# Inverse square roots of four groups moved from GpSimd to a Newton batch on VectorE

## The chip, the cores and the metric

The kernel runs on one core of a Trainium2 chip. The metric is the device time of one execution in microseconds, the median of several runs. TensorE is written PE in the profile, VectorE DVE, ScalarE ACT, GpSimd POOL and SyncE SP.

## The reference

`x` is 16 x 256 rows of 128 numbers (4096 rows). Three layers follow one another, all in float32:

```python
x = x + 0.5 * ffn(layernorm(x))
x = x + attn(layernorm(x))
x = x + 0.5 * ffn(layernorm(x))

# layernorm: (x - mean) / sqrt(var + 1e-5), over the 128 numbers of a row
# ffn: logits = x @ router.T, one of 8 experts by argmax;
#      y  = (silu(x @ gate_e.T) * (x @ up_e.T)) @ down_e.T    (the row's expert, hidden width 256)
#      ys = the same with the shared expert's weights, for every row;  y + ys
# attn: circular convolution with a key, decaying sum over the 256 rows of a sequence,
#       circular correlation with a second key; x + gate * result
```

## The kernel before

The 4096 rows are 32 tiles of 128 rows, in eight groups of four tiles (`G` = 8, `TPG` = 4). The two feed-forward layers are numbered f = 0 and f = 1. Each has a loop over the groups that normalizes, routes and sends the rows out, and then a loop over 39 blocks of 128 rows of one expert each (`experts`).

**The opening (f = 0).** Every engine runs its own program and they meet at semaphores. Step k of `front(0, k)` does this. VectorE chooses the expert of each row of group k from the router's product (`choose`, L646 to L652); between the links of that chain it places the first half of the statistics of group k + 3 (`moments`, L575), and behind it their end (`aggregate`, L582 to L586). TensorE then counts ranks (L924 to L932), and VectorE turns them into the row's slot (`place_rows`, L661 and L665). GpSimd sends each tile of the group to its slots by an indirect DMA (`scatter`, L391), four to a group. GpSimd also turns variances into inverse square roots, by a power of minus a half (`rstd`, L376), and makes the shift from it (L380): groups 0, 1 and 2 ahead of the first scatter, groups 3 and 4 in one instruction ahead of the scatters of group 1, 5 and 6 ahead of those of group 3, and 7 ahead of those of group 4. ScalarE copies the transposed rows out of PSUM (L475), normalizes the next group (`norm`, L460), and does the SiLUs (L484). TensorE's order in step k is: a piece of the shared expert, the router's product for group k (L902), another piece, the transposes of group k + 1 (L867), the ranks of group k.

**The shared expert** is cut into pieces `(g, part)`: parts 0 and 1 are the two halves of gate and up of group g (L881 on TensorE, the SiLU L484, the product `mult` L623 on VectorE), and part 2 (`DOWN`) the down product (L889) and its addition to the rows (`add_shared`, L591). They are worked off in the order of `SHARED_PARTS`: none in step 0, two in each of the steps 1 to 7 (`PER_STEP`), five behind the last step (`parts_left`), and the last five, (6,1), (7,0), (6,2), (7,1), (7,2), behind the loop over blocks.

**The end of the opening.** VectorE writes `pad_row` (L729) behind the slots of group 7 and then makes the tables of blocks (L742 to L768). SyncE writes eight blocks of pads to the rows that `pad_row` names (L331), and waits for the tables, all pads and all 32 scatters (L336) before it loads the first blocks (L320).

**Preparing the attention** (`prepare_attention`, L831 to L839; a product L1000 on TensorE; a Tanh L551 on ScalarE) stands in step 0.

**Behind the blocks of f = 0.** SyncE waits for all rows that GpSimd returned and loads them into `back`. VectorE does the products of (6,1) and (7,0) and the addition of (6,2), then in `middle(-4)` adds `back` of group 0 (L591), takes its statistics for the attention, and does the product of (7,1); in `middle(-3)` it does the same for group 1, and then the addition of (7,2). `middle(-2)` begins with the scan of group 0 (L603). TensorE does its five pieces and then the transposes for that scan (L867), which need ScalarE's normalized rows (L460).

## Time and profile before

| | |
|---|---|
| median of 3 runs | 306.56 us (306.52 to 307.95) |
| the profiled execution | 306.67 us, its span 304.9 us |
| mean granted TensorE clock | 0.924 of full speed |
| busy, share of the span | PE 85%, DVE 60%, POOL 57%, ACT 53% |

Times in a profile count from the start of the span; the profiled execution's own time is 1.8 us longer than its span. A timeline row gives start, duration, engine, line and operation, what is written and read, how many instructions are merged in the row, and in brackets the idle time ahead of it and what ended that. `issue` is time in which an engine waited for nothing that the profile shows.

### The profile page before, as it was taken

Reading aid. Unit: us, or ns where it says so; the run is one execution under the profiler, and the core shown is the slowest. Engines: PE = TensorE matmul, PEld = TensorE weight load, DVE = VectorE, ACT = ScalarE, POOL = GpSimd, SP = SyncE. Lnnn points to the kernel's source line nnn. Section 1 sums busy time; section 2 is a strip of 40 time slices with the busy share of each in tenths; the row PEclk is TensorE's granted clock in tenths of the full one; section 3 lists DMA queues with packets and bytes.
Section 4 is the critical chain, followed back from the end, with each engine's and each line's share of the span. In section 5 each row is a group of like instructions: output and inputs, shape, how many; then the busy total and the mean of one; then the engine's idle time right before and its main releaser. Section 6 shows DMA issues by size and latency. Waiting matters only on the chain.

```text
span 304.9 us, 6662 instructions
## 1 busy us (share of the span) xinstructions
PE 259.1 (85%) x1802; PEld 213.1 (70%) x1802; DVE 184.4 (60%) x752; ACT 160.4 (53%) x374; POOL 172.7 (57%) x223
## 2 busy tenths in 40 slices
PE   8789999839999999857698999999940999999980
PEld 2457677529999999636465676666620899999980
DVE  4647656724566556357999788784471266666650
ACT  2635542226777677118485776654202477767730
POOL 6467787701667667713543667665653047477673
PEclk9899999978999999996597999999995699999996
DMA  6961112433333321054000111121263835444110
GB/s 198 342 256 48 42 47 64 141 80 75 89 92 93 83 63 43 30 153 123 0 2 1 53 41 49 71 72 70 72 211 108 212 93 148 132 113 136 38 54 9
DMA packets 27060, 28.56 MB, mean 94 GB/s; under 512 B 4711, under 2 KB 23533, under 8 KB 26768
## 3 DMA queue, kind: packets, MB, share of 16 engines
q1 hardware_dynamic: 21968, 17.51, 20.5%
q0 software_dynamic: 5056, 10.63, 10.2%
q8 instruction: 15, 0.25, 0.4%
q14 instruction: 21, 0.17, 0.2%
HBM read 15.70 MB, written 13.34 MB: 95 GB/s over the span
## 4 chain that ended last, share of the span: by engine, by line
PE 54%; POOL 15%; issue 12%; DVE 9%; DMA 6%; ACT 3%; POOLq 0%; SPq 0%; DVEq 0%; ACTq 0%
PE bank L956 21%; PE bank L881 10%; POOL dispatched L391 9%; PE bank L966 9%; PE bank L889 5%; PE bank L947 3%; PE bank L908 2%; PE bank L902 2%; DVE scanned L603 2%; POOL returned L418 2%; POOL scale_f L376 2%; DMA dispatched<-rows,slot 2%; DVE st_f L575 1%; POOL out L418 1%; DMA xs<-dispatched 1%
## 5 line engine op out<-in xcount | busy, mean ns | idle before, releaser
L956 PE MATMUL bank<-xsT,wgu 128*128 128x128 f32 x624 | 86.1, 283 | 1.2 <-ACT xsT L530 1.2
L391 POOL DMA_INDIRECT dispatched<-rows,slot x64 | 63.1, 987 | 30.8 <-issue 18.3
L956 PEld LDWEIGHTS bank<-xsT,wgu 128*128 128x128 f32 x624 | 79.2, 199 | 1.7 <-issue 1.7
L881 PE MATMUL bank<-xnT,gu 128*128 128x512 f32 x128 | 64.2, 629 | 2.2 <-DVE hs L623 1.8
L800 DVE TENSOR_TENSOR eh<-eg,bank 128x256 f32<-128x256 f32 x78 | 32.9, 422 | 46.1 <-ACT eg L537 45.5
L418 POOL DMA_INDIRECT out<-ey,token x39 | 38.3, 981 | 30.6 <-DVE ey L809 19.8
L418 POOL DMA_INDIRECT returned<-ey,token x39 | 38.3, 982 | 30.5 <-DVE ey L813 18.1
L509 ACT ACTIVATE wgu<-gu 128x512 f32 x78 | 48.3, 624 | 9.7 <-DVE tab_row L768 6.3
L484 ACT ACTIVATE sg<-bank 128x512 f32<-128x512 f32 x32 | 19.0, 593 | 56.6 <-PE bank L881 56.6
L966 PE MATMUL bank<-wdn,eh 128*128 128x128 f32 x312 | 47.1, 276 | 0.8 <-DVE ey L809 0.4
L537 ACT ACTIVATE eg<-bank 128x256 f32<-128x256 f32 x78 | 29.9, 383 | 33.2 <-PE bank L956 32.5
L966 PEld LDWEIGHTS bank<-wdn,eh 128*128 128x128 f32 x312 | 40.8, 192 | 1.1 <-DVE eh L800 1.1
L889 PEld LDWEIGHTS bank<-dn,hs 128*128 128x128 f32 x256 | 32.3, 201 | 12.5 <-DVE hs L623 8.5
L889 PE MATMUL bank<-dn,hs 128*128 128x128 f32 x256 | 33.5, 287 | 5.9 <-DVE hs L623 5.9
L881 PEld LDWEIGHTS bank<-xnT,gu 128*128 128x128 f32 x128 | 22.8, 197 | 20.6 <-issue 19.6
L460 ACT ACTIVATE rows<-rows,shift_f,scale_f 128x128 f32<-128x128 f32 x64 | 26.3, 484 | 14.6 <-POOL shift_f L380 14.6
L947 PE MATMUL bank<-ident,xs 128*128 128x128 f32 x78 | 16.6, 291 | 14.4 <-DMA xs<-dispatched 14.4
L777 DVE COPY wdn<-dn 128x256 f32 x78 | 23.5, 303 | 5.6 <-issue 4.6
L623 DVE TENSOR_TENSOR hs<-sg,bank 128x512 f32<-128x512 f32 x32 | 21.8, 681 | 8.1 <-ACT sg L484 8.0
L376 POOL TENSOR_TENSOR scale_f<-var_f,minus_half 128x4 f32<-128x4 f32 (+1 forms) x14 | 15.6, 1113 | 12.2 <-DVE minus_mean_f L586 12.1
L902 PEld LDWEIGHTS bank<-routerT,xnT 128*128 128x128 f32 x128 | 16.2, 194 | 7.7 <-issue 3.9
L947 PEld LDWEIGHTS bank<-ident,xs 128*128 128x128 f32 x78 | 10.8, 152 | 15.2 <-issue 14.5
(99 smaller groups left out, 299.8 us busy)
## 6 DMA issues: line engine op xcount, KB each, us to landing
xs<-dispatched SPq DMA_DIRECT2D x39, 130.0 KB, 2.2
xs<-dispatched SPq DMA_DIRECT2D x39, 66.0 KB, 2.1
gu<-in_gu SPq DMA_DIRECT2D x1, 2048.0 KB, 10.8
back<-returned SPq DMA_DIRECT2D x8, 256.0 KB, 5.3
dispatched<-pads SPq DMA_DIRECT2D x9, 130.0 KB, 3.0
dn<-in_dn SPq DMA_DIRECT2D x1, 1024.0 KB, 11.6
dispatched<-rows,slot POOLq DMA_INDIRECT x64
returned<-ey,token POOLq DMA_INDIRECT x39, 2.3
```

What stands on the lines that cost most here:

```text
L391: nc.gpsimd.indirect_dma_start(dispatched[f][:, :], bass.IndirectOffsetOnAxis(slot[:, i:i + 1], 0), rows[:, i, 0:width(f)], None, bounds_c ...
L418: nc.gpsimd.indirect_dma_start(target, bass.IndirectOffsetOnAxis(token[:, b % TR:b % TR + 1], 0), ey[:, b % YR, :], None, bounds_check=las ...
L460: nc.scalar.activation(dst[:, at * TPG + t, 0:C], xres[:, i, :], ACT.Identity, bias=shift[kind][:, i:i + 1], scale=scale[kind][:, i:i + 1] ...
L509: nc.scalar.activation(wgu[:, b % GR, :], tile(gu, expert_of(digits[0], b)), ACT.Copy).then_inc(blk_wgu, 1)
L537: nc.scalar.activation(eg[:, b % GR, :], bank[4 + b % GR][:, 0:H], ACT.Silu).then_inc(blk_silu, 1)
L777: nc.vector.tensor_copy(wdn[:, b % WR, :], tile(dn[:].rearrange("p e h c -> p e (h c)"), expert_of(digits[0], b))).then_inc(blk_wdn, 1)
L800: nc.vector.tensor_tensor(eh[:, b % WR, :], eg[:, b % GR, :], bank[4 + b % GR][:, H:2 * H], ALU.mult).then_inc(blk_mul, 1)
L881: last = nc.tensor.matmul(ps[:], gu[:, SHARED, at:at + P], xnT[:, g, :], start=True, stop=True)
L889: last = nc.tensor.matmul(o_ps[:, t * C:(t + 1) * C], hs[:, n % 2, h, t * P:(t + 1) * P], dn[:, SHARED, h, :], start=(h == 0), stop=(h == ...
L947: last = nc.tensor.transpose(bank[q % 2][:, i * P:(i + 1) * P], xs[:, b % XR, 0:C], ident[:])
L956: last = nc.tensor.matmul(bank[4 + b % GR][:, c * P:(c + 1) * P], wgu[:, b % GR, c * P:(c + 1) * P], xsT[:, b // 2 % TURNS, b % 2, :], sta ...
L966: last = nc.tensor.matmul(bank[2 + b % 2][:, 0:C], eh[:, b % WR, h * P:(h + 1) * P], wdn[:, b % WR, h * C:(h + 1) * C], start=(h == 0), st ...
```

## The change

Groups 4 to 7 of the opening no longer get their inverse square roots from GpSimd's power. VectorE computes all sixteen columns at once behind the slots of group 2: a first guess from the bits of the number, three Newton steps of three instructions, and the shift, twelve instructions in a chain, each waiting for the one before. GpSimd keeps groups 0 to 3, all ahead of its first scatter. For this the statistics of group 5 move into step 1, and those of groups 6 and 7 into step 2 (`STATS_AT`). ScalarE's `norm` of groups 4 to 7 waits for the whole chain. The attention's preparation moves from step 0 to step 3 (`PREPARE_AT`) on all engines, and TensorE waits for the shared weights behind the router's product of group 0 instead of ahead of it. `FILL` gives the same two pieces to each step as `PER_STEP` did. The last five pieces (`REST`) keep their order; on VectorE the product of (7,1) now stands ahead of `middle`, and the addition of (7,2) in `middle(-4)`.

```diff
+STATS_AT = {-3: (0,), -2: (1,), -1: (2,), 0: (3,), 1: (4, 5), 2: (6, 7)}
+BY_DVE = 4
+NEWTON = 3
+MAGIC = float(0x5F3759DF)
+DVE_RSTD_STEPS = 3 + 3 * NEWTON
+SHARED_FROM = 1
+PREPARE_AT = 3
...
-PER_STEP = 2
-EARLY = PER_STEP * (G - 1)
+FILL = (0, 2, 2, 2, 2, 2, 2, 2)
+EARLY = sum(FILL)
 LATE = EARLY + 5
+REST = SHARED_PARTS[LATE:]
+REST_DVE = {-4: REST[4:6], -3: REST[6:7], -2: REST[7:]}
...
             def first_ffn(k):
                 if k < 0:
-                    rstd("f", k + AHEAD, k + AHEAD)
-                elif k in (1, 3):
-                    rstd("f", k + 2, k + 2, groups=2)
-                elif k == 4:
-                    rstd("f", k + 3, k + 3)
-                if valid(k):
+                    rstd("f", k + BY_DVE, k + BY_DVE)
+                else:
                     scatter(0, k)
...
-                act.wait_ge(rstd_done[kind], (n + 1) * RSTD_STEPS)
+                if kind == "f" and BY_DVE <= n < G:
+                    act.wait_ge(dve_rstd, DVE_RSTD_STEPS)
...
+            def rstd_of_rest():
+
+                at = slice(BY_DVE * TPG, NT)
+                v, y, step = var["f"][:, at], scale["f"][:, at], [0]
+
+                def link(ins):
+                    step[0] += 1
+                    ins.then_inc(dve_rstd, 1)
+                    if step[0] < DVE_RSTD_STEPS:
+                        dve.wait_ge(dve_rstd, step[0])
+
+                dve.wait_ge(stats["f"], G)
+                link(nc.vector.tensor_scalar(square[:].bitcast(I32), v.bitcast(I32), 1, None,
+                                             ALU.logical_shift_right))
+                link(nc.vector.tensor_scalar(y.bitcast(I32), square[:].bitcast(I32), -1.0, MAGIC, ALU.mult, ALU.add))
+                for _ in range(NEWTON):
+                    link(nc.vector.tensor_tensor(square[:], y, y, ALU.mult))
+                    link(nc.vector.scalar_tensor_tensor(out=square[:], in0=square[:], scalar=-0.5, in1=v,
+                                                        op0=ALU.mult, op1=ALU.mult))
+                    link(nc.vector.scalar_tensor_tensor(out=y, in0=square[:], scalar=1.5, in1=y,
+                                                        op0=ALU.add, op1=ALU.mult))
+                link(nc.vector.tensor_tensor(shift["f"][:, at], y, minus_mean["f"][:, at], ALU.mult))
...
                 if valid(k):
                     place_rows(n, k, q)
+                for more in laters[1:]:
+                    stats_of(kind, more, more)
+                if f == 0 and k == max(STATS_AT):
+                    rstd_of_rest()
...
-                if k < -2:
-                    shared(0, *SHARED_PARTS[k + 2])
+                for g, part in REST_DVE.get(k, ()):
+                    shared(0, g, part)
...
-                if k == 0:
+                if k == PREPARE_AT:
                     prepare_attention()
...
-            for g, part in SHARED_PARTS[LATE:-2]:
+            for g, part in REST[:4]:
                 shared(0, g, part)
...
             pe.wait_ge(routes_in, 16)
+            for k in range(0, SHARED_FROM):
+                front(0, k)
             pe.wait_ge(shared_in, 16 * 2)
-            front(0, 0)
+            for k in range(SHARED_FROM, PREPARE_AT + 1):
+                front(0, k)
             pe.wait_ge(small_in, 16 * 4)
```

## Rows read from the trace of the kernel before

**Rows 1.** Timeline of GpSimd in the opening: powers and scatters.

```profile
13.39 1.20 POOL L391 DMA_INDIRECT dispatched<-rows,slot  x1 [2.17 <-DVE slot L665]
...
19.90 1.67 POOL L376 TENSOR_TENSOR scale_f<-var_f,minus_half 128x8 f32<-128x8 f32 x1 [1.48 <-DVE minus_mean_f L586]
...
22.41 1.07 POOL L391 DMA_INDIRECT dispatched<-rows,slot  x1 [0.49 <-issue]
...
39.85 1.05 POOL L376 TENSOR_TENSOR scale_f<-var_f,minus_half 128x4 f32<-128x4 f32 x1
...
41.34 1.05 POOL L391 DMA_INDIRECT dispatched<-rows,slot  x1 [0.16 <-issue]
...
59.28 0.97 POOL L391 DMA_INDIRECT dispatched<-rows,slot  x1 [0.30 <-issue]
```

**Rows 2.** Chain that ended last, 0 to 75 us: start, us, what.

```profile
60.55 2.32 DMA dispatched<-rows,slot
...
66.83 2.05 PE bank L956 x8
```

**Rows 3.** Timeline of VectorE and TensorE in steps 0 to 3 of the opening.

```profile
12.61 0.17 DVE L586 TENSOR_SCALAR minus_mean_f<-mv_f 128x4 f32<-128x4 f32 x1
...
12.74 3.45 PE L881 MATMUL bank<-xnT,gu 128*128 128x512 f32 x4
...
26.28 0.19 DVE L665 TENSOR_REDUCE slot<-place 128x4 int32<-128x32 f32 x1
...
28.22 1.96 PE L881 MATMUL bank<-xnT,gu 128*128 128x512 f32 x4
...
31.28 2.05 PE L889 MATMUL bank<-dn,hs 128*128 128x128 f32 x16 [0.51 <-DVE hs L623]
...
31.36 0.19 DVE L665 TENSOR_REDUCE slot<-place 128x4 int32<-128x32 f32 x1
```

**Rows 4.** Timeline of VectorE: a choice without statistics, and a piece of the tables.

```profile
44.36 0.19 DVE L646 TENSOR_REDUCE top<-bank 128x4 f32<-128x32 f32 x1 [1.59 <-PE bank L902]
...
45.64 0.68 DVE L623 TENSOR_TENSOR hs<-sg,bank 128x512 f32<-128x512 f32 x1
...
55.91 0.20 DVE L762 SCALAR_TENSOR_TENSOR blk_row<-block_no,blk_from 128x40 f32<-128x40 f32 x1
...
56.14 0.20 DVE L764 TENSOR_TENSOR packed<-blk_exp,digit 128x40 f32<-128x40 f32 x1
```

**Rows 5.** The pads: timeline of `pad_row`, and line 331 from 48 to 62 us.

```profile
51.74 0.16 DVE L729 TENSOR_TENSOR pad_row<-bank,pad_base 128x8 int32<-128x8 f32 x1
...
L331 SPq DMA_DIRECT2D dispatched<-pads x8: 332/332/354, 53.9 to 58.1; - x8
...
DMA to landing us min/median/max: 1.9/2.3/2.6
```

**Rows 6.** Stretches of 1 us: PE, PEld, DVE, ACT, POOL, clock, DMA.

```profile
13.00:14.00 1.00, 1.00 (x2) 0.33 (x1) 0.91 (x5) 0.42 (x2) 0.61 (x1) 0.50 1.05 442
...
136.00:137.00 1.00, 0.00 (x0) 0.00 (x0) 0.93 (x9) 0.00 (x0) 0.00 (x0) 0.50 0.95 266
...
163.00:164.00 1.00, 1.00 (x5) 0.60 (x4) 1.00 (x8) 0.66 (x2) 0.00 (x0) 0.55 0.02 8
```

**Rows 7.** Timeline behind the first blocks, 133 to 143 us.

```profile
133.59 0.60 ACT L484 ACTIVATE sg<-bank 128x512 f32<-128x512 f32 x1 [2.91 <-PE bank L881]
134.63 0.69 DVE L591 SCALAR_TENSOR_TENSOR rows<-back,rows 128x512 f32<-128x512 f32 x1 [2.06 <-DMA back<-returned]
...
136.82 0.68 DVE L623 TENSOR_TENSOR hs<-sg,bank 128x512 f32<-128x512 f32 x1
...
137.56 3.79 PE L889 MATMUL bank<-dn,hs 128*128 128x128 f32 x16 [4.00 <-DVE hs L623]
...
138.51 1.65 ACT L460 ACTIVATE xa<-rows,shift_a,scale_a 128x128 f32<-128x128 f32 x4 [4.32 <-POOL shift_a L380]
...
142.24 1.22 DVE L603 TENSOR_TENSOR_SCAN scanned<-keep,bank 128x512 f32<-128x512 f32 x1 [0.16 <-PE bank L867]
```

More of the change, by code:

```diff
@@ L137, in build @@
         scale_more = sb("scale_more", [P, NT])
+        square = sb("square", [P, (G - BY_DVE) * TPG])
         top = sb("top", [P, TPG])
@@ L252, in parts_at @@
             if f == 0:
-                return SHARED_PARTS[PER_STEP * (k - 1) + i:][:1] if 1 <= k < G else []
+                if not valid(k):
+                    return []
+                first, middle = sum(FILL[:k]), (FILL[k] + 1) // 2
+                return SHARED_PARTS[first + i * middle:first + (FILL[k] if i else middle)]
             if not valid(k):
@@ L368, in _, with rstd @@
             last_token = pool.to_reg(N - 1)
-            def rstd(kind, n, k, groups=1):
-                s, w = rstd_done[kind], groups * TPG
-                at = slice(k * TPG, k * TPG + w)
-                pool.wait_ge(stats[kind], n + groups)
+            def rstd(kind, n, k):
+                s = rstd_done[kind]
+                at = slice(k * TPG, (k + 1) * TPG)
+                pool.wait_ge(stats[kind], n + 1)
+                if kind == "f" and n >= G:
+                    pool.wait_ge(dve_rstd, DVE_RSTD_STEPS)
+                    n -= G - BY_DVE
                 sc = scale[kind][:, at]
-                nc.gpsimd.tensor_tensor(sc, var[kind][:, at], minus_half[:, 0:w], ALU.pow).then_inc(s, 1)
+                nc.gpsimd.tensor_tensor(sc, var[kind][:, at], minus_half[:], ALU.pow).then_inc(s, 1)
                 pool.wait_ge(s, n * RSTD_STEPS + 1)
@@ L442, in _ @@
             pool.wait_ge(const_made, 3)
-            for k in range(-AHEAD, 1):
-                first_ffn(k)
-            for k in range(1, G):
+            for k in range(-BY_DVE, G):
                 first_ffn(k)
@@ L556, in _, with middle @@
             experts(0)
-            for g, part in SHARED_PARTS[LATE:]:
+            for g, part in REST[:6]:
                 shared(0, g, part)
-            steps(lambda k: front(1, k), 3)
+            def middle(k):
+                front(1, k)
+                for g, part in REST_PE.get(k, ()):
+                    shared(0, g, part)
+            steps(middle, 3)
             before_experts(1)
@@ L668, in front @@
                 n, q = f * G + k, k % 2
-                kind, later = ("f", k + AHEAD) if f == 0 else ("a", k + 4)
+                kind, laters = ("f", STATS_AT.get(k, ())) if f == 0 else ("a", (k + 4,))
+                later = laters[0] if laters else G
                 if f == 0 and valid(later):
@@ L718, in middle @@
                 front(1, k)
-                if k < -2:
-                    shared(0, *SHARED_PARTS[k + 2])
+                for g, part in REST_DVE.get(k, ()):
+                    shared(0, g, part)
             def pads_behind(f):
@@ L1006, in _, with middle @@
             experts(0)
-            for g, part in SHARED_PARTS[LATE:]:
+            for g, part in REST[:6]:
                 shared(0, g, part)
             pe.wait_ge(setup, 6)
-            steps(lambda k: front(1, k), 3)
+            def middle(k):
+                front(1, k)
+                for g, part in REST_PE.get(k, ()):
+                    shared(0, g, part)
+            steps(middle, 3)
             for g, part in parts_left(1):
```

14 lines of the change are left out of this document (10 added, 4 removed).

## The prediction

> **What bounds the kernel now.** I read the chain of waits first, for the opening. From about 20 to 61 us it is one unbroken run of GpSimd scatters: each takes 0.97 us plus 0.30 us until the next [rows 1], so 32 of them need 41 us. Three times the run is broken by an inverse square root of L376. Group 0's four scatters (first at 13.39) are out at about 18.5, but the next starts at 22.41, behind the 1.67 us power of groups 3 and 4: 3.9 us. The same power stands once more at 32.4 (2.2 us lost), and the one at 39.85 costs 1.2 us [rows 1]. Together that is 7.3 us, and it is what the change goes for. The last scatter's rows land at 62.87, and only then does SyncE load the experts' first blocks [rows 2].
>
> Next, the order of time on TensorE and VectorE, because a scatter also needs its slots. Slots of group 2 are written at 26.47, those of group 3 at 31.55 [rows 3]; GpSimd without its powers would want group 3's at about 31. So this second chain (gate-up, router product, gate-up or down, transposes, ranks, slots: about 5.0 us a step) is almost as late as GpSimd. A third one hangs on it: VectorE's pad rows at 51.74, then SyncE's eight pad writes from 53.9 to 58.1, each landing 2.3 us after its issue (1.9 to 2.6), the last at 60.4 [rows 5]. SyncE waits for pads and scatters alike. The opening can therefore give at most 62.87 - 60.4 = 2.5 us, whatever GpSimd gains, unless the slots come earlier, and the change doesn't make them earlier.
>
> Last, the stretch after the first experts, where the diff also moves two VectorE pieces: it is bound by a chain of waits through `back`, VectorE, TensorE and the first scan [rows 7].
>
> **The change part by part.** *GpSimd.* Three powers leave it; the one of group 3 now stands ahead of the first scatter. Its statistics are ready at 12.77 [rows 3]; from power to scatter takes 1.49 us, as from 39.85 to 41.34 [rows 1], which puts the first scatter at 14.4 in place of 13.39. Cover: group 1's slots come at 20.7, four scatters end at 19.6, so this costs nothing.
>
> *Steps 0 to 2.* The attention's preparation leaves step 0, where VectorE had been idle behind it. It frees TensorE by 0.3 us; group 2's slots go from 26.47 to about 26.1. Group 5's statistics move into step 1 and group 6's into step 2, group 7's behind the slots of step 2: 1.49 us for a group (136.82 less 134.63 + 0.70) [rows 7].
>
> *Newton steps.* Twelve dependent instructions on 128x16. The trace has none of that width. From below: six linked steps of a choice take 1.28 us (44.36 to 45.64), 0.21 each; from above: the table's chain steps by 0.23 us (55.91 to 56.14) on 40 columns [rows 4]. I take 0.21, so 2.5 us (range 2.5 to 2.8). They have no cover: VectorE is at 26.1 with group 2's slots, 27.6 with group 7's statistics, and 30.1 with the last shift. Behind them wait, on VectorE, the add of group 0 (0.6) and the choice of step 3, which TensorE has had ready since 28.0; on ScalarE, the normalizing of group 4, and queued behind it both SiLUs of step 3; on TensorE, the transposes of group 4 and all that follows. In numbers: choice 30.7 to 32.0; ScalarE normalizes 30.1 to 31.7 (1.65 [rows 7], the next can start 0.1 sooner), SiLU to 32.2; product to 32.95; slots of group 3 at 33.4 instead of 31.55; the down product of group 1, which waits for that product, at 33.0 instead of 31.28 [rows 3]. So the slot chain is 1.7 us later, and GpSimd idles from 31.2 to 33.7.
>
> *TensorE's clock.* Between the gate-up of step 3 (28.22 before [rows 3], now about 27.9, done in 2.0) and 33.0 TensorE has only four transposes and the ranks: a hole of 3.3 us. The trace shows what such holes do. The granted clock is at half (1.2 GHz) at 13, after sparse small work; at 136, 2.4 us after 133.6; and at 163 after a stretch that was only thinned by waits [rows 6]. At half, a group of four gate-up products takes 3.45 us [rows 3] instead of 1.96 [rows 3], and the low stretches that were filled with work lasted about 3.4 us (13 to 16.4). I charge one such stretch: 1.7 us more on the slot chain. From the down product (31.28) to the pad rows (51.74) TensorE is the pace and nothing there is changed but the preparation (1.6 us of VectorE at step 3, hidden while TensorE does the down product and the router). So the pad rows stand at 33.0 + 20.46 + 1.7 = 55.1, the last pad at 63.8 less 0.2 for a wait on ScalarE in step 4 that goes: 63.5. GpSimd's last scatter lands at about 62. The gate for the experts is now the pads, at 63.5: **+0.65** against 62.87. Without the fall it is 61.8: -1.1.
>
> *Start of the experts.* Blocks begin at 66.83 at the half clock, 2.05 us for eight matmuls [rows 2]. TensorE's leftover products now end 3.2 us later, so the fall comes later, and less of the blocks' work is done slow. Between 0 and 2.0; I take **-0.35**, which lets the low stretch end where it ended.
>
> *Statistics, choice and shared parts later.* Steps 3 and 4 have no statistics left; VectorE isn't the pace there. Zero. The wait for the shared weights moves behind the first router product: they had landed, zero.
>
> *After the experts.* `REST` has five parts; by its slices the product (7,1) now stands before the first add of `back`, and the add of group 7 behind the first statistics instead of behind the second add. Before, the SiLU of (7,1) is ready at 134.19, VectorE idles until `back` comes (134.63, 2.06 us idle), adds, does statistics, and multiplies only at 136.82; TensorE, its clock down, takes 3.79 us for the down product from 137.56; its queue holds the transposes for the scan behind that, though their input is ready at 140.16; the scan starts at 142.24 [rows 7]. Now: product 134.2 to 134.9, `back` added 0.2 later, down product 134.9 to 137.7 at the latest, its add on VectorE 0.7, which lies in VectorE's wait. The transposes follow ScalarE: 140.4, scan at 140.75. **-1.5**. From the scan to 154.6 VectorE is the chain, without a gap, then TensorE; both keep the 1.5.
>
> Sum: 0.65 - 0.35 - 1.5 = -1.2 against the profiled execution's 306.67 (span 304.9 plus 1.8): 305.5. The median is 0.1 lower: **305.4**.
>
> **The rivals.**
> - *No fall of the clock in the hole* (A). For it: the transposes and ranks lie in the hole. Then -1.1 at the gate, and TensorE is so close behind its leftover work that the experts may start at the full clock: -1.1 - 0.35 to -1.1 - 2.0, and -1.5: 302.0 to 303.6, say 302.6.
> - *A low stretch elsewhere falls away* (B). The one at 163 lies in a part that TensorE bounds; 1.2 us of shift can give its sparse moment more work. 305.4 - 1.7 = 303.7. As well one can be added: 307.1 (B').
> - *The moved product gives nothing* (C): `back`, not the product, could hold the scan through ScalarE. 305.4 + 1.5 = 306.9. Against it: 2.1 us between ScalarE's 140.16 and the scan.
> - *Slower: Newton's steps are held up beside the scatters* (D). Group 2's scatters run during them. The nearest rows say no: 0.2 us steps and 0.97 us scatters stand side by side in the tables' chain [rows 1, 4]. From above: if a step could run only in the 0.30 us between scatters, 2.5 us would become up to 10.7. The price is one to one on slots and pads. From 2.7 us more the kernel is over 308.1; I put it at 309.
> [...]
> - *The change does what it is for* (E): slots keep pace, opening -2.5, 302.6 with the rest. The 2.5 us of uncovered Newton speak against it.
>
> **How the numbers follow.** Forecast 0.34 (own range 304.6 to 306.4); A 0.13; B 0.17; B' and C 0.19, of it 0.06 for both at once (308.6); D 0.12, of it 0.09 above 308.1; E 0.05. Range: 302.5 to 307.7; what is left out is D, B' with C, and the lower edge of A and E. Half a per cent, about what a measurement of this kernel tells from no change, is 1.5 us: 305.0 to 308.1. Faster: A, B, E and a sixth of the forecast: 0.41. Slower: 0.09 and 0.06, 0.15. Same: 0.44.
>
> **What would show it.** Right: no L376 between scatters; twelve steps in 2.5 us; scatter of group 3 near 33.7 after an idle of 2.4 us; granted clock at half for one stretch after about 33; the last pad, not the last scatter, releasing the first block load, at 63 to 64; the scan 1.5 us nearer to the landing of `back`. Wrong: steps of over 0.3 us (D), full clock through 33 to 37 (A), a scan that comes as late as before behind `back` (C), a missing low stretch past 160 (B).

## The result, and the profile after

| | before | changed |
|---|---|---|
| median (us) | 306.66 | 311.07 |
| lowest to highest | 306.52 to 307.95 | 309.58 to 312.04 |
| profiled execution, span | 306.67, 304.9 | 312.04, 310.3 |
| mean granted clock | 0.924 | 0.904 |

The changed kernel takes 1.0137 of the time before, 95% interval 1.0088 to 1.0186: it is slower by 1.4%. A second set of runs gave 310.97 against 307.03, 1.0112 (1.0069 to 1.0155). The forecast was 305.4, with a range up to 307.7. Ratios, here and below, leave out executions more than 1.5% above the fastest of the same kernel, so a ratio is not the quotient of the two medians (they lie up to 0.5% apart).

I cut both executions at events that both have, which shows where the time came in. The third kernel is the changed one once more, profiled in the second set (`e5_changed_again`). It matters because the first step of the opening differs between executions without any cause in the code.

| us | before | changed | changed again |
|---|---|---|---|
| slots of group 1 written | 20.7 | 22.8 | 21.0 |
| slots of group 2 | 26.5 | 28.2 | 26.7 |
| group 2 to group 3 | 5.1 | 7.2 | 7.2 |
| group 3 to group 4 | 5.7 | 7.0 | 8.7 |
| slots of group 7 written | 51.8 | 57.2 | 57.3 |
| from there to the first block load | 11.2 | 10.0 | 9.9 |
| first block load | 63.07 | 67.14 | 67.21 |
| from there to the load of `back` | 68.6 | 69.2 | 68.2 |
| load of `back` to the first scan | 10.6 | 9.3 | 9.3 |
| first scan to fifth scan | 29.6 | 31.8 | 31.7 |
| fifth scan to the end of the span | 133.1 | 132.8 | 132.6 |

Against "changed again" the span grows by 4.1: 4.1 at the gate of the experts, -0.4 in the blocks, -1.3 to the scan, +2.1 behind it, -0.5 in the rest. Against the first execution of the changed kernel it is 5.4. There 2.1 us more than before stand at the slots of group 1 already, ahead of everything that the Newton steps could delay.

The page of the changed kernel: TensorE's busy tenths and its granted clock, in 40 slices of 7.8 us.

```profile
PE   7799899959999999885698999999960799999990
...
PEclk9759799995999999998558999999995599999996
```

The clock row of the page before, in slices of 7.6 us:

```profile
PEclk9899999978999999996597999999995699999996
```

The clock row is lower in the second, third and fifth slices (11.7 to 21.9 and 35.5 to 39.0 us), and from 145 to 162 us. Now the opening itself. VectorE, ScalarE and TensorE in the timeline of the changed kernel (start, length, engine, line, operation, tile; in brackets the idle time ahead and what ended it):

```profile
28.01 0.19 DVE L711 TENSOR_REDUCE slot<-place 128x4 int32<-128x32 f32 x1
...
29.70 0.18 DVE L624 TENSOR_SCALAR square<-var_f 128x16 int32<-128x16 int32 x1
29.91 0.17 DVE L626 TENSOR_SCALAR scale_f<-square 128x16 int32<-128x16 int32 x1
...
32.00 0.17 DVE L633 TENSOR_TENSOR shift_f<-scale_f,minus_mean_f 128x16 f32<-128x16 f32 x1
...
32.21 1.65 ACT L477 ACTIVATE rows<-rows,shift_f,scale_f 128x128 f32<-128x128 f32 x4 [4.15 <-DVE shift_f L633]
...
35.11 3.40 PE L940 MATMUL bank<-dn,hs 128*128 128x128 f32 x16 [0.40 <-DVE hs L669]
...
35.19 0.19 DVE L711 TENSOR_REDUCE slot<-place 128x4 int32<-128x32 f32 x1
```

The Newton chain runs from 29.70 to 32.17, twelve steps that start 0.21 us apart. ScalarE waits 4.15 us for its last product. The down product behind it takes 3.40 us, where it took 2.05 before [rows 3]: the fall of the clock has come. Slots of group 3 are written at 35.38, 7.2 us behind those of group 2.

GpSimd in the same timeline (it answers to [rows 1]):

```profile
28.47 0.97 POOL L409 DMA_INDIRECT dispatched<-rows,slot  x1 [0.56 <-DVE slot L711]
...
35.65 0.97 POOL L409 DMA_INDIRECT dispatched<-rows,slot  x1 [2.39 <-DVE slot L711]
...
42.70 0.97 POOL L409 DMA_INDIRECT dispatched<-rows,slot  x1 [2.26 <-DVE slot L711]
...
55.51 0.97 POOL L409 DMA_INDIRECT dispatched<-rows,slot  x1 [2.90 <-PE bank L953]
...
64.54 0.97 POOL L409 DMA_INDIRECT dispatched<-rows,slot  x1 [0.30 <-issue]
```

In [rows 1] powers stand between the scatters; here there are none, and GpSimd idles instead. It waits 2.39 and 2.26 us for slots and then 2.90 us for something else: a router product of TensorE (L953). The last scatter starts at 64.54, and in the chain of waits it is this one that the block loads follow, no pad (start, length, what; it answers to [rows 2]):

```profile
64.54 2.40 DMA dispatched<-rows,slot
...
70.85 2.05 PE bank L1007 x8
```

Behind the first experts, in the timeline of the changed kernel (it answers to [rows 7]):

```profile
138.99 0.69 DVE L669 TENSOR_TENSOR hs<-sg,bank 128x512 f32<-128x512 f32 x1 [1.66 <-ACT sg L501]
...
139.73 2.05 PE L940 MATMUL bank<-dn,hs 128*128 128x128 f32 x16 [1.41 <-DVE hs L669]
...
143.47 1.65 ACT L477 ACTIVATE xa<-rows,shift_a,scale_a 128x128 f32<-128x128 f32 x4 [4.51 <-POOL shift_a L398]
...
144.10 1.54 PE L918 MATMUL bank<-ident,xa 128*128 128x128 f32 x4 [2.32 <-ACT xa L477]
...
145.68 1.22 DVE L649 TENSOR_TENSOR_SCAN scanned<-keep,bank 128x512 f32<-128x512 f32 x1 [0.98 <-PE bank L918]
```

The down product of (7,1) is done at 141.8, in 2.05 us, not 3.79 as in [rows 7]. TensorE then has nothing for 2.32 us, and the scan follows ScalarE. The windows behind the scan show what comes next (stretch, length, busy us of PE, PEld, DVE, ACT, POOL, then granted clock, DMA share, GB/s). The changed kernel:

```profile
147.00:154.00 7.00, 4.62 (x19) 3.92 (x20) 6.73 (x28) 3.83 (x11) 2.96 (x5) 0.50 0.00 0
154.00:161.00 7.00, 7.00 (x28) 5.69 (x28) 6.66 (x36) 6.01 (x16) 3.04 (x5) 0.50 0.01 2
```

The kernel before, the same stretches:

```profile
147.00:154.00 7.00, 5.25 (x24) 3.87 (x22) 6.72 (x31) 4.38 (x12) 3.63 (x7) 0.58 0.00 0
154.00:161.00 7.00, 6.42 (x38) 4.13 (x37) 6.76 (x34) 5.98 (x16) 3.64 (x7) 1.00 0.01 2
```

From 154 to 161 TensorE is busy without a gap at the half clock (1.2 GHz); before, it had the full one (2.4 GHz). So there are four suspects: the Newton chain, the fall of the clock behind it, GpSimd's wait for the router product, and the low clock behind the moved product. Each of the first experiments takes one.

### The profile page after: what moved, and what is told of

The parts are those of the page before. It is cut to its first block, busy times and chain, and to the rows that moved or that the text cites. A ratio compares the mean times of both kernels' runs of the same rounds, so it can differ in the third digit from the quotient of the medians.

```text
span 310.3 us, 6675 instructions
## 1 busy us (share of the span) xinstructions
PE 266.4 (86%) x1802; PEld 218.0 (70%) x1802; DVE 187.8 (61%) x764; ACT 160.3 (52%) x374; POOL 168.7 (54%) x219
## 4 chain that ended last, share of the span: by engine, by line
PE 68%; DVE 9%; issue 7%; POOL 6%; ACT 4%; DMA 4%; POOLq 0%; SPq 0%; DVEq 0%; ACTq 0%
PE bank L1007 22%; PE bank L932 16%; PE bank L1017 10%; PE bank L940 7%; PE bank L953 5%; PE bank L959 3%; POOL dispatched L409 3%; PE bank L998 3%; PE bank L918 2%; POOL out L432 2%; DVE scanned L649 2%; DMA dispatched<-rows,slot 2%; DVE st_f L598 1%; DMA xs<-dispatched 1%; ACT xnT L492 1%
## 5 line engine op out<-in xcount | busy, mean ns | idle before, releaser
L932 PE MATMUL bank<-xnT,gu 128*128 128x512 f32 x128 | 66.9, 651 | 1.4 <-DVE hs L669 1.0
L851 DVE TENSOR_TENSOR eh<-eg,bank 128x256 f32<-128x256 f32 x78 | 32.9, 421 | 47.2 <-ACT eg L554 46.0
L932 PEld LDWEIGHTS bank<-xnT,gu 128*128 128x128 f32 x128 | 24.0, 207 | 20.7 <-issue 20.7
L477 ACT ACTIVATE rows<-rows,shift_f,scale_f 128x128 f32<-128x128 f32 x64 | 26.3, 484 | 12.6 <-POOL shift_f L398 8.4
L669 DVE TENSOR_TENSOR hs<-sg,bank 128x512 f32<-128x512 f32 x32 | 21.8, 683 | 10.9 <-ACT sg L501 10.5
L998 PE MATMUL bank<-ident,xs 128*128 128x128 f32 x78 | 16.7, 292 | 13.2 <-DMA xs<-dispatched 13.1
L953 PEld LDWEIGHTS bank<-routerT,xnT 128*128 128x128 f32 x128 | 18.0, 213 | 7.6 <-issue 3.9
L953 PE MATMUL bank<-routerT,xnT 128*128 128x8 f32 x128 | 18.1, 268 | 2.8 <-ACT xnT L492 2.4
L998 PEld LDWEIGHTS bank<-ident,xs 128*128 128x128 f32 x78 | 10.7, 151 | 14.0 <-issue 10.7
## 6 DMA issues: line engine op xcount, KB each, us to landing
gu<-in_gu SPq DMA_DIRECT2D x1, 2048.0 KB, 10.7
dn<-in_dn SPq DMA_DIRECT2D x1, 1024.0 KB, 11.2
```

Source lines behind the costliest of these rows:

```text
L477: nc.scalar.activation(dst[:, at * TPG + t, 0:C], xres[:, i, :], ACT.Identity, bias=shift[kind][:, i:i + 1], scale=scale[kind][:, i:i + 1] ...
L851: nc.vector.tensor_tensor(eh[:, b % WR, :], eg[:, b % GR, :], bank[4 + b % GR][:, H:2 * H], ALU.mult).then_inc(blk_mul, 1)
L932: last = nc.tensor.matmul(ps[:], gu[:, SHARED, at:at + P], xnT[:, g, :], start=True, stop=True)
L953: last = nc.tensor.matmul(rt[:, t * E:(t + 1) * E], xnT[:, k, t * P:(t + 1) * P], routerT[:], start=True, stop=True)
L998: last = nc.tensor.transpose(bank[q % 2][:, i * P:(i + 1) * P], xs[:, b % XR, 0:C], ident[:])
```

## The experiments

The runs are called e1 to e16 in the order in which they were made, and the recorded expectations count them so: the third experiment is e3. They were made in four sets, e1 to e4, e5 to e8, e9 to e12 and e13 to e16, and each ratio is against the kernel before in the same set. The stage times are those of one profiled execution of each kernel.

In the edits, `fill` issues matmuls on a tile of ones into a PSUM bank that nobody reads at that moment; they compute nothing that is used:

```python
def fill(to, count):
    for _ in range(count):
        nc.tensor.matmul(to[:], warm[:, 0:P], warm[:], start=True, stop=True)
```

### The Newton chain

```diff
-NEWTON = 3
+NEWTON = 0
```

> The changed kernel with the three Newton steps left out (nine of the twelve chained VectorE instructions; the first guess from the bits and the shift stay), so that its inverse square roots are only the rough guess. Theory 1, the chain is uncovered and every microsecond of it is paid at least once: nine steps of 0.21 us are 1.9 us, the slots of group 3 come 1.9 us earlier than the changed kernel's 35.4, TensorE's hole in step 3 shrinks from about 2.5 us to under 1 us, and the time is 309.1 or less against 311.1. Theory 2, the loss is in TensorE's low clock alone, which begins before the Newton steps (11.7 to 21.9 us in the changed kernel's profile): the time stays within 1 us of 311.

Measured (e1): 305.91 against 307.05, ratio 0.9979 (0.9942 to 1.0016). The kernel leaves out the nine Newton instructions, so it only shows what they cost. Slots of group 3 follow those of group 2 after 5.3 us (7.2 with the chain, 5.1 before), and group 4 after 5.4. With the length of the chain its price on the slots goes, and the low stretch behind it too.

### The fall of the clock behind it

Eleven matmuls ahead of the transposes of step 3, in the changed kernel:

```diff
+                if f == 0 and k == 3:
+                    for _ in range(11):
+                        nc.tensor.matmul(bank[1][:], warm[:, 0:P], warm[:], start=True, stop=True)
```

> The changed kernel with eleven matmuls of the warm-up kind (bfloat16, 512 columns, into a bank that nobody reads) ahead of the transposes of step 3, in TensorE's hole. They do no useful work. Theory 2, the hole costs a low stretch of the clock: the granted clock stays at full from 35.8 to 39.2 us, the router's product of group 4 starts 1.5 us earlier, and the time falls by 1 to 2 us. Theory 1 alone, the hole costs only its own length: the clock may stay up but slots of group 7 and the time move by less than 0.5 us, or get worse if the matmuls outlast the hole.

Measured (e2): 306.32, ratio 1.0002 (0.9964 to 1.004). Group 2 to group 3 stays 7.2, group 3 to group 4 goes from 7.0 (or 8.7) to 5.4. The windows at the same place show why, first the changed kernel:

```profile
36.00:40.00 4.00, 4.00 (x22) 3.76 (x22) 1.65 (x7) 0.93 (x3) 3.09 (x4) 0.63 0.15 51
```

then the changed kernel in the second set, where the low stretch lasted from 34.3 to 41.1:

```profile
36.00:40.00 4.00, 4.00 (x14) 2.98 (x14) 1.44 (x8) 0.00 (x0) 2.35 (x3) 0.50 0.15 51
```

and with the hole filled:

```profile
36.00:40.00 4.00, 4.00 (x31) 2.98 (x31) 2.86 (x11) 1.16 (x3) 3.09 (x4) 1.00 0.15 51
```

TensorE is shown as busy for all of the four microseconds in each; what differs is the clock, and with it how many matmuls get done. The fall costs 1.6 us on the slots when it lasts 3.4 us and 3.3 when it lasts 6.8. I had charged 1.7. The gate opens at 65.13, 2 us earlier.

### GpSimd's wait

In `scatter(0, 6)` GpSimd waits for the router product of group 7 (L388 and L389 of the kernel before; the diff leaves them alone, and so did my sum). Without that wait, in the changed kernel:

```diff
-                elif k == G - 2:
-                    pool.wait_ge(logits, k + 2)
```

> The changed kernel without GpSimd's wait for the router's product of group 7 ahead of the scatters of group 6 (only order, no data). In the changed kernel's profile GpSimd stands 2.9 us there although the slots of group 6 are written 3 us before, and the last scatter, not the pads, opens the gate. Theory 3, this wait has become part of the loss: the last scatter starts at 61.8 in place of 64.5, the gate is then the pads at about 65.9 instead of 67.1, and the time falls by about 1.2 us. Rival: the scatters of group 6 only come closer to TensorE's work and the pads, no change within 0.4 us.

Measured (e4): 307.28, ratio 1.0021 (0.9978 to 1.0064). From the slots of group 7 to the first block load it takes 8.5 us instead of 9.9 to 10.0, and the pads are what opens the gate, as the forecast had it. GpSimd doesn't stop ahead of group 6, and the chain of waits goes through the pads:

```profile
51.74 0.98 POOL L407 DMA_INDIRECT dispatched<-rows,slot  x1 [0.30 <-issue]
...
62.09 2.17 DMA dispatched<-pads
```

So the wait costs 1.4 us at the gate. The median fell by more, 3.7 us, and the rest isn't the wait's: in the profiles another 1.7 us against "changed again" is a low stretch behind the chain of 3.4 us instead of 6.8, which this edit doesn't touch.

The wait was there before and cost nothing. Before, GpSimd was behind: group 6's slots were written at 47.2, but the first of its scatters started at 51.6, and the router product of group 7 had ended at 49.4. In the changed kernel GpSimd has caught up with the slots. It could send group 6 at 52.5, and the router product runs from 53.76 to 54.72:

```profile
53.76 0.96 PE L953 MATMUL bank<-routerT,xnT 128*128 128x8 f32 x8
```

### The moved product alone

The kernel before, with only the VectorE product of (7,1) ahead of the first `back` and the addition of (7,2) behind the first statistics:

```diff
-                if k < -2:
-                    shared(0, *SHARED_PARTS[k + 2])
+                if k == -4:
+                    shared(0, *SHARED_PARTS[-1])
...
-            for g, part in SHARED_PARTS[LATE:-2]:
+            for g, part in SHARED_PARTS[LATE:-1]:
```

> The kernel before with one part of the change alone: on VectorE the product of (7,1) ahead of the first add of back, and the addition of (7,2) one step earlier. Opening untouched. If the last part of my sum stands (1.5 us predicted, 1.3 us between the back load and the scan in the two profiles), the scan of group 0 starts 1.3 to 1.5 us earlier and the time is 305.2. Rival: the gain is lost again in the attention's steps, where TensorE's clock is low at other moments; then 306 to 307.

Measured (e3): 308.33, ratio 1.0057 (1.0020 to 1.0095). This part alone, which I had at -1.5 us, brings no gain. That it makes the kernel slower is less sure than the interval suggests: over all executions of the two kernels in this set the means differ by 0.3%, where single ones of the kernel before spread by 1.9%. So I go by the stages. The scan is nearer to the load of `back`, 9.3 us as in the changed kernel, and the stretch from the first to the fifth scan is 31.3 (29.6 before), together 40.6 instead of 40.2:

```profile
136.57 2.05 PE L889 MATMUL bank<-dn,hs 128*128 128x128 f32 x16 [1.41 <-DVE hs L623]
...
140.94 1.54 PE L867 MATMUL bank<-ident,xa 128*128 128x128 f32 x4 [2.33 <-ACT xa L460]
```

Its windows, 0.50 and 0.70 where the kernel before has 0.58 and 1.00:

```profile
147.00:154.00 7.00, 5.39 (x22) 3.91 (x20) 6.73 (x33) 4.01 (x11) 3.45 (x9) 0.50 0.00 0
154.00:161.00 7.00, 7.00 (x24) 4.94 (x25) 6.43 (x30) 4.18 (x12) 3.76 (x6) 0.70 0.01 2
```

This run also has a first low stretch of 10.2 us (11.4 to 21.7), although its opening is that of the kernel before, where it lasted 3.4. So a first stretch of that length comes without the change, and the 2.1 us at group 1 in the first table need not be the change's: here the slots of group 1 stand at 22.9.

### Is it the clock?

The same kernel with matmuls to fill TensorE's idle moments there: ten ahead of the first step of the attention's loop, five ahead of a piece and five ahead of the transposes in the next two.

```diff
+                if f == 1 and k < 0:
+                    fill(bank[4], 10 if k == -3 else 5)
...
+                if f == 1 and -3 < k < 0:
+                    fill(bank[4], 5)
```

> The kernel before with the moved two pieces of shared work behind the experts (as in the third experiment) and with matmuls of the warm-up kind in TensorE's idle stretches from the down product of group 7 to the router of group 0 (ten, then four times five, into a bank that nobody reads). Theory 2, the moved product does bring the scan 1.5 us forward, but TensorE, done 2 us sooner, idles longer and its clock stays low until 158 to 161 us in place of 152.8, so that the gain is lost before the fourth scan: here the clock stays at full, from the back load to the fifth scan it takes 38.5 us in place of 40.2 (before) and 40.6 (moved pieces alone), and the time is 2 us under that of the third experiment. Rival: VectorE is the pace up to the fourth scan whatever the clock: 40 us again.

Measured (e7): 303.44, ratio 0.9883 (0.9842 to 0.9923). From the load of `back` to the fifth scan: 38.4 us, against 40.2 before and 40.6 with the moved product alone.

```profile
147.00:154.00 7.00, 5.58 (x25) 2.93 (x25) 6.45 (x32) 4.10 (x12) 3.65 (x9) 0.85 0.00 0
154.00:161.00 7.00, 6.63 (x31) 4.54 (x30) 5.69 (x27) 4.45 (x13) 2.36 (x5) 0.91 0.01 2
```

The clock stays up for most of these windows. The profiled stage gains 2.2 us against the moved product alone, while the medians differ by 4.9. Most of the rest lies between the executions: the profiled one (306.32, clock 0.940, first low stretch 10.2 us) is the slowest of its six, and four of them ran in 303.3 to 303.5 at a clock of 0.957.

The steps from scan to scan in several profiles, with and without fillers, show where the clock costs time. Times are counted from the first scan; all kernels but the one before have the moved product.

| us | clock low | scan 2 to 3 | scan 3 to 4 | scan 4 to 5 | first to fifth |
|---|---|---|---|---|---|
| before | up to 0.4; 3.8 to 10.7; 20.9 to 24.3 | 5.6 | 7.6 | 10.9 | 29.6 |
| changed again | -1.2 to 15.9; 22.7 to 26.1 | 5.6 | 9.6 | 10.9 | 31.7 |
| e1 | -1.2 to 15.9 | 5.6 | 9.3 | 9.2 | 29.7 |
| e4 | -1.9 to 18.6 | 5.6 | 10.9 | 9.2 | 31.3 |
| e7 | 9.2 to 12.6 | 7.0 | 7.6 | 9.2 | 29.3 |
| e9 (below) | none | 5.5 | 7.6 | 9.2 | 27.8 |

The step from the third to the fourth scan takes 7.6 us where the clock is up and 9.3 to 10.9 where it is still low. That is the 2.1 us that the changed kernel loses here. The step behind it takes 10.9 where a stretch of 3.4 us falls into it and 9.2 where none does; the kernel before has that one too. So the order on VectorE is not what costs here; e16 (below) has the old order and a full clock behind the scan, and takes as long from the first to the fifth scan as e10 with the new one, 28.1 us. What the moved product would be worth at a full clock isn't shown: no kernel with the fillers keeps the old order undisturbed.

The same fillers in the changed kernel, which otherwise keeps its chain, its hole and its wait:

> The changed kernel with one remedy alone: the matmuls of the warm-up kind in TensorE's idle stretches of the attention's first steps. Theory 2: of the 4 us that the change loses, the longer low clock behind the experts is 2.2 us (back load to fifth scan 41.0 against 38.4 with fillers), so 308 to 308.8 us; the rest, the hole of step 3 and the wait ahead of the scatters of group 6, stays. Rival: the middle is worth nothing when the opening is late: 310 or more.

Measured (e13): 307.41, ratio 0.9987 (0.9954 to 1.0021). By the ratios this is 1.2% under the changed kernel of the second set. The profile doesn't show where it comes from. Up to 161 us the clock behind the scan is low for 3.4 us, where the changed kernel's is for 17.0, and yet the load of `back` to the fifth scan takes 40.4 us and not the 38.4 that I expected: one stretch of 3.4 us lengthens the step from the second to the third scan to 7.0, and another the one from the fourth to the fifth to 10.9. That execution (310.76) is the slowest of twelve.

### Another place for the chain

If the chain stands where its cover is missing, it should be moved. With all statistics in steps 0 and 1 it runs behind the slots of group 1:

```diff
-STATS_AT = {-3: (0,), -2: (1,), -1: (2,), 0: (3,), 1: (4, 5), 2: (6, 7)}
+STATS_AT = {-3: (0,), -2: (1,), -1: (2,), 0: (3, 4, 5, 6), 1: (7,)}
...
+                    dve.wait_ge(x_in[3], 16)
```

> The changed kernel with the same work in another place: the statistics of groups 4 to 6 behind the slots of group 0, where VectorE idles 4.7 us in the changed kernel (all of x has landed by 12.8), those of group 7 in step 1, and the Newton chain behind the slots of group 1. Nothing is left out. Theory 1, the loss is the chain's place and not the chain: no idle of GpSimd ahead of the scatters of group 3, their slots near 33 in place of 35.4, no hole of TensorE in step 3 and no low clock behind it; the time is 2 to 3 us under the changed kernel's of this call. Rival: the chain now delays step 2 by as much, slots of group 2 later by 2 us, no gain.

Measured (e6): 307.28, ratio 1.0021 (0.9985 to 1.0057), 3.7 us better than the changed kernel. Group 2 to 3 takes 5.0, 3 to 4 takes 5.3, without a low stretch; group 1 to 2 takes 6.1. The first block load is at 63.49, against 63.07 before.

One thing about these single remedies (e1, e2, e4, e6, e13): against the changed kernel each lowers the ratio by 0.9 to 1.6%, the whole loss or nearly, and together they would be worth several times what the change lost. So their medians can't be added up. The remedies overlap, and the clock differs also where an edit doesn't touch it: e4, which fills nothing, ran at 0.919 in the median, the changed kernel at 0.909 and 0.912 in its two sets. How the loss is shared out I therefore read from the stages of the profiles alone.

### All repairs together, and the change weighed against the kernel before

The kernels of this part have the fillers of the attention's loop, no wait of GpSimd for the router product of group 7, and in the opening four matmuls ahead of the router product of group 0 and four ahead of its ranks:

```diff
+                if n == 0:
+                    fill(bank[7], 4)
```

With the early chain:

> An attempt at a version that beats both: the changed kernel with statistics and Newton chain early (as in the sixth), without GpSimd's wait ahead of the scatters of group 6 (as in the fourth), with matmuls of the warm-up kind in TensorE's idle stretches of step 0 (twice four) and of the attention's first steps (as in the seventh). Theory 2 with theory 1: slots of group 7 at 51 to 52, low clock behind 12 us gone, gate at 61 to 62, and 302 us. Rival, the fillers stand in the way of TensorE's own work in step 0 and shift everything by up to 1.7 us: 305 us.

Measured (e8): 301.96, ratio 0.9806 (0.9751 to 0.986). Once more, in the next set, beside the two kernels that follow:

> The kernel of the eighth experiment unaltered, to stand beside the others of this call on one chip: 302.0 us again, within 0.7.

Measured (e11): 302.08, ratio 0.9886 (0.9818 to 0.9954). The two ratios of this one kernel differ by 0.8%, so ratios from different sets are not told apart by less than that.

The kernel before with the moved product and the same repairs. It has everything but the Newton batch and what goes with it (the places of the statistics and of the attention's preparation):

> The kernel before, with its powers on GpSimd, and with everything that the eighth experiment adds beside the Newton chain: the moved two pieces, no wait ahead of the scatters of group 6, matmuls of the warm-up kind in step 0 and in the attention's first steps. With the clock treated alike this shows what the Newton batch itself is worth. Theory 1 with the chain early: GpSimd's three powers cost 2 to 2.5 us at the gate (first block load near 63 against 62.2 in the eighth, where the pads open it), so 302.5 to 303.5 us against 302.0. Rival, the slots and pads are the pace in both and the chain is worth nothing: 302.

Measured (e9): 302.79, ratio 0.9887 (0.9805 to 0.9969). First block load at 61.79, low stretches only at 63.0 to 69.8, at 223.4 to 237.1 and at the end.

The changed kernel, its chain where it stands, with the same repairs and eleven matmuls in the hole:

> The changed kernel with the Newton chain where the change put it (behind the slots of group 2) and every clock remedy: matmuls of the warm-up kind in step 0, in the hole of step 3 and in the attention's first steps, and no wait ahead of the scatters of group 6. Theory 1: with the clock up the late chain still costs its 2.1 us on the slots of group 3 and so on the pads: gate at 63.5 to 64, 303.5 to 304.5 us, 1.5 to 2 over the kernel with the early chain. Theory 2 alone: as fast as the early chain, 302.

Measured (e10): 299.84, ratio 0.9785 (0.9727 to 0.9843), under what either theory expected. First block load at 60.46, where I had 63.5 to 64; the slots of group 2 stand at 24.4 here, against 28.5 and 29.2 in e8 and e11. In its timeline the fillers lie in the hole (ten of them have a record), the slots of group 3 still come 7.4 us behind those of group 2, and GpSimd still waits for them:

```profile
28.13 2.32 PE L913 MATMUL bank<-warm 128*128 128x512 bf16 x10
...
31.57 0.19 DVE L709 TENSOR_REDUCE slot<-place 128x4 int32<-128x32 f32 x1
...
32.03 0.97 POOL L407 DMA_INDIRECT dispatched<-rows,slot  x1 [2.18 <-DVE slot L709]
```

In its chain of waits the gate is now the pads:

```profile
58.04 2.27 DMA dispatched<-pads
...
61.01 1.79 DMA xs<-dispatched
```

With the clock held up, the change is worth 1.3 us at the gate (60.46 against 61.79) and 1% of the time (299.84 against 302.79 in the same set). The two intervals overlap a little, but five of the six executions of e10 are faster than all of e9. The sign has turned.

The early chain, which had helped the changed kernel, is slower here by 2.2 us (302.08 against 299.84 in the same set). Its slots of group 1 come at 22.2 instead of 18.6, with its statistics ahead of the choice of step 1. But the comparison isn't of the place alone: e10 has its hole filled, and e11 keeps a low stretch in step 1 (21.7 to 25.2). The runs that follow show what the place is worth otherwise. With neither filled (e14 against e11) there is no difference, 301.85 and 302.08, and with both filled (e15 against e12) the late chain is 0.5 us ahead at the gate, 60.49 against 60.95; the medians are 2.1 us apart there, in two sets, and 1.1 us of it is a low stretch that only the profile of e12 has between its scans (147.2 to 150.6). So my account of e6, that only the place was wrong, falls in that form: the early place helps where it avoids the hole, and no more once the hole is filled.

The same kernel without the eleven in the hole:

```diff
-                if f == 0 and k == 3:
-                    fill(bank[1], 11)
```

> The kernel of the tenth experiment (late chain, all remedies) without the eleven matmuls in the hole of step 3. The hole's own price in a kernel that is otherwise undisturbed. Theory 2: one low stretch of 3.4 us from about 31 to 34, slots of group 4 later by 1.7 us, pads and gate too: 301.5 us against 299.8. Rival: GpSimd's scatters or luck hide it: 300.

Measured (e14): 301.85, ratio 0.9823 (0.9777 to 0.9868), in the set behind that of e10. The low stretch is back (31.7 to 35.2), group 3 to group 4 is 7.0 instead of 5.4, and the first block load 62.01 instead of 60.46. By the profile the hole costs 1.6 us once more; by the medians 2.0, or by the ratios 0.4%, with intervals that overlap. With its hole unfilled the kernel has no lead at the gate over e9 (62.01 against 61.79), so the lead of 1.3 us that e10 has there comes with the filled hole.

And e10 without the moved product:

```diff
-REST_DVE = {-4: REST[4:6], -3: REST[6:7], -2: REST[7:]}
+REST_DVE = {-4: REST[3:4], -3: REST[4:5], -2: REST[7:]}
...
-            for g, part in REST[:4]:
+            for g, part in REST[:3]:
```

> The kernel of the tenth experiment with VectorE's product of (7,1) and the addition of (7,2) back where the kernel before had them. Price of that part of the change with the clock held up. If the moved product is worth its 1.3 us up to the first scan and nothing takes it back: 301.1 us. Rival: with the fillers the down product of group 7 runs at the full clock anyway, the gain was only the low clock's: 300 within 0.4.

Measured (e16): 302.58, ratio 0.9846 (0.9793 to 0.99). The first scan comes 13.1 us behind the load of `back`. This run doesn't answer its question: ten fillers stood behind the late down product and ran in part at the half clock (137.2 to 139.9, the clock back at 138.4), which delays the transposes by themselves.

### More filling

A few matmuls at the start of the two loops over blocks, where the page shows low clocks too:

```diff
+                fill(bank[6], 42 if f else 6)
...
+                fill(bank[6], 4)
```

With the early chain, and eight more in step 1:

> The kernel of the eighth experiment with more matmuls of the warm-up kind: eight in TensorE's wait of step 1, six ahead of and four behind the first block's transposes of f = 0, 42 and four at those of f = 1, where TensorE idles 10.3 us. Theory 2: the low stretches at 21 to 25, 66 to 69 and 226 to 236 us shrink or go, 1.7 us at each of the two block starts, so 298.5 to 300 us. Rival: the fillers outlast the idle time and delay the blocks: 302 or more.

Measured (e12): 300.33, ratio 0.9806 (0.9746 to 0.9867). With the chain where the change has it:

> The kernel of the tenth experiment with the fillers of the twelfth at the two block starts as well. In the twelfth they took the low stretches there away. 3 to 4 us of half clock at the first start and 4 us at the second are 1.7 and 2 us of work: 296.5 to 298 us. Rival: transfers, not TensorE, are the pace at the block starts: 299.5.

Measured (e15): 298.23, ratio 0.9708 (0.9661 to 0.9756). Its page, busy tenths and clock:

```profile
PE   6999999899999999888898999999988999999980
...
PEclk9999999999999999999999999999999999999997
```

Apart from the end there is no low stretch left. This kernel beats the one before by 2.9%, and by the ratios the changed one by 4%. Of the 2.9%, 1.1% are in e9 already, which has GpSimd's powers; 1.0% is what e10 has over e9; the last 0.8% came with the fillers at the block starts, and is no more than two sets differ. The kernel before with all of these fillers wasn't run, so what the change is worth in the best kernel stays open.

The repetition of the changed kernel, by which the first result was confirmed:

> The changed kernel once more, unaltered, beside the kernel before on the same chip. Single executions of one kernel spread by over 5 us here, and the four of the changed kernel may have met unlucky moments of TensorE's clock. Theory 2, part of the 4.4 us is such luck (in its profile the clock is low from 11.7 to 21.9 us, in that of the kernel before only from 12.9 to 16.3, though the code up to there is nearly the same): the median lies 1 to 2.5 us over the kernel before. Theory 1, everything is the change's own: 4 us or more again.

Measured (e5): 310.97, ratio 1.0112 (1.0069 to 1.0155). The difference is 3.9 us, next to what theory 1 expected; the first low stretch lasts 6.8 us in this profile, 10.2 in the first.

## Why the prediction was wrong

**The Newton chain.** Right. 2.47 us at 0.21 a step; slots of group 3 were 7.3 behind those of group 2 in the forecast and are 7.2. Rival D, which would have stretched the chain beside scatters, fell: the steps keep 0.21 us and the scatters 0.97. The Trainium skill, SBUF — State Buffer, section "SBUF: two separate sides", says that a VectorE instruction with two SBUF inputs and a GpSimd instruction that reads SBUF exclude each other for the whole instruction. Ten of the twelve steps have two such inputs, and no exclusion shows between them and the scatters; whether a scatter counts as an instruction that reads SBUF is not shown here.

**TensorE's clock in the hole.** The fall came, so rival A fell; the term for it, 1.7 us, was only the lower of two prices. I charged one low stretch, 1.7 us; two executions show 7.0 and 8.7 us from group 3 to group 4 against 5.4 filled, so 1.6 or 3.3. Filling the hole alone brought the ratio from 1.0137 and 1.0112 down to 1.0002.

**What opens the gate.** Wrong, by a wait that I didn't list. The forecast had the last scatter at about 62 and the pads at 63.5. GpSimd's wait for the router product of group 7 was hidden before by GpSimd's own backlog, and this backlog was what the change removed. The step that failed is "GpSimd's last scatter lands at about 62": I counted its scatters and powers, but not the waits in its code. The wait is worth 1.4 us by the run without it. Of the 3.7 us between the forecast gate (63.5) and that of the second execution (67.21), 1.4 are this wait, 1.7 the longer low stretch (8.7 us from group 3 to group 4, where a short one gives 7.0), and 0.6 the slots of group 2, at 26.7 instead of 26.1. The run without the wait bears out the rest of this sum: with a short low stretch and the slots of group 2 at 27.0, 0.9 late, its pads open the gate at 64.42, also 0.9 late.

**Start of the experts.** Forecast -0.35, measured -0.4 between the first load and that of `back` in the second execution and +0.6 in the first: not told apart from noise.

**The moved product.** The first half was right: forecast -1.5, measured -1.3 up to the scan. The second half, "both keep the 1.5", is the other step that failed: +2.1 by the fifth scan, so the stage costs 0.8 us where the forecast had -1.5. I had seen that TensorE would finish early, and priced what it does early, but not what its clock does when it then has nothing to do. In the kernel before, the down product at the half clock ran into the transposes, and the clock came back at 142.6 and again at 152.8. In the changed kernel, 2.32 us without work come ahead of the transposes, and the clock is low from 144.8 to 161.8. That the low clock is the cause, and not the order on VectorE, is shown by the table of the scans: with the same order the step from the third to the fourth scan takes 7.6 us at the full clock (e7, e9) and 9.3 to 10.9 at the half.

**The rivals.** I had a missing low stretch (B) and an added one (B'), 1.7 us each, as mishaps that might cancel; the changed kernel has added ones at two places, and longer. E (the change does what it is for) fell with the slots of group 3. C gave the right sign for the stage (the moved product gives nothing) by the wrong cause: `back` didn't hold the scan. The sum of the misses, second execution: 3.5 at the gate (+4.1 for +0.65), 2.3 behind the experts (+0.8 for -1.5), -0.5 in the rest: 5.3, as +4.1 stands to -1.2.

**What stays open.** Why the first low stretch lasts 3.4 us in one execution and 10.2 in another of the same code: single executions of the kernel before spread from 303.2 to 309.1 us, and the slower ones show in the main a lower mean clock (0.940 to 0.908 in all). Why a second stretch of 3.4 us behind the scans is there in some executions (before, changed, e3, e13) and not in others (e1, e2, e4, e6). What each single remedy is worth by itself, since their medians don't add up. And how much of the 1% in e10 against e9 is the change itself, since e10 also has the hole filled and the two intervals overlap.

## What to carry to other kernels

When a change takes work off an engine that runs behind, read the code of that engine for every wait between there and the gate: those that its backlog hid open up together. When it makes TensorE finish sooner and then wait, or adds a chain that TensorE must sit out, price what follows at the half clock for longer than the shortest low stretch that the trace shows, and test the change with the hole filled by matmuls that nobody reads: here that alone took it from 1.1 to 1.4% slower to no difference. And before a gain of 1% is judged from two profiles, compare by stage, since low stretches that neither version causes move a single execution by more than that.

## What the hardware showed that I had not expected

- Low stretches of the clock were from 3.4 to 20.5 us long, and the same code showed 3.4 in one execution and 10.2 in another. In the profile of before they sum to 46.3 us, in the changed kernel's to 59.7, in the best one's only the end is left (4.1), with a mean granted clock of 0.993 and a span of 295.4.
- Filling cost little where TensorE was idle. The best kernel issues 105 matmuls more, of which its profile shows 100 (1902 instead of 1802); ten of them take 2.3 us at full clock, and in e10 they lie in time that was idle. In e16 they stood in the way.
- In the hole, where TensorE is what the slots wait for, a low stretch cost about half of its length: 3.4 us of it 1.6, 6.8 us 3.3. Behind the experts, where VectorE is the pace for a while, 17.1 us of it cost 1.7 to 2.1.
